# Neighbourhood attention on one Trainium2 core: P is turned and scaled by a product with a diagonal matrix

## The reference

```
q = (gn(x) @ Wq + bq).reshape(B, nh, H, W, lr) * scale      # nh = 8 heads, lr = 4
k = (gn(x) @ Wk + bk).reshape(B, nh, H, W, lr)
v = (gn(x) @ Wv + bv).reshape(B, nh, H, W, hd)              # hd = 32
...
attn = jnp.einsum('bhijc,bhikjlc->bhijkl', q, k_win)        # 7 x 7 keys of each query
attn = attn + bias
attn = jax.nn.softmax(attn.reshape(B, nh, H, W, K * K), axis=-1)
out = jnp.einsum('bhijkl,bhikjld->bhijd', attn, v_win)
x = x + out @ Wp + bp
```

## Time and profile before

| | us |
|---|---|
| median of 3 runs | 10392.46 |
| lowest and highest | 10381.14, 10393.34 |
| span of the profiled execution | 10375.5 |
| `layer0_attend`, clearing of `qn` to last transposes, in it | 374.5 to 2483 |
| PE busy over the span | 8825.9 (85%) |
| DVE, ACT, POOL busy | 5783.3, 4145.5, 3261.0 |
| TensorE clock granted, mean over the span | 0.809 of 2.4 GHz |

### The profile page before, as it was taken

The page is one execution under the profiler, slowest core; times in us unless marked ns, Lnnn a source line. Parts: engine busy times, 40 slices in busy tenths (PEclk is TensorE's granted clock), DMA queues, the critical chain, the costliest instruction groups (busy, mean ns, idle before and its releaser), DMA issues. The chain is left out here.

```text
span 10375.5 us, 158377 instructions
## 1 busy us (share of the span) xinstructions
PE 8825.9 (85%) x47072; PEld 4663.3 (45%) x47072; DVE 5783.3 (56%) x13683; ACT 4145.5 (40%) x9073; POOL 3261.0 (31%) x1854
## 2 busy tenths in 40 slices
PE   4499989997667999998999989999999885448888
PEld 3355545554444444444444444444444334325555
DVE  4355555555557976675766757766676004324444
ACT  1255555553000055555555555555555660001111
POOL 2000000000000055555555555555555670142211
PEclk8655555555876599999999999999999996569999
DMA  4511121101533001202112021111211004211110
GB/s 137 88 20 20 20 35 20 20 8 49 178 123 103 10 20 28 56 21 56 27 24 56 19 56 30 31 45 30 47 28 41 14 5 127 78 40 42 44 34 21
DMA packets 368839, 480.22 MB, mean 46 GB/s; under 512 B 154040, under 2 KB 322362, under 8 KB 354855
## 3 DMA queue, kind: packets, MB, share of 16 engines
q1 hardware_dynamic: 344551, 426.24, 17.0%
q0 software_dynamic: 23424, 43.45, 1.6%
HBM read 298.80 MB, written 180.34 MB: 46 GB/s over the span
## 5 line engine op out<-in xcount | busy, mean ns | idle before, releaser
L1057 POOL TENSOR_TENSOR a_added<-a_P 128x896 f32<-128x896 f32 x1344 | 2805.3, 2107 | 3517.1 <-ACT a_P L1029 3516.8
L935 DVE TENSOR_REDUCE a_tops<-a_ps 128x1 f32<-128x448 f32 x5600 | 3166.2, 632 | 1322.8 <-PE a_ps L843 1319.5
L1029 ACT ACTIVATE a_P<-a_ps 128x448 f32<-128x448 f32 (+1 forms) x5600 | 2610.3, 548 | 2600.3 <-PE a_ps L901 2599.3
L901 PE MATMUL a_ps<-a_qp,a_kp 98*128 98x448 f32 (+1 forms) x5600 | 1946.8, 399 | 171.4 <-DMA a_qp<-scratch_neg 97.9
L843 PE MATMUL a_ps<-a_hk,a_hq 96*128 96x448 f32 (+1 forms) x4900 | 1922.6, 406 | 118.9 <-DMA a_hk<-scratch_k 96.8
L843 PEld LDWEIGHTS a_ps<-a_hk,a_hq 96*128 96x128 f32 (+1 forms) x4900 | 917.7, 188 | 1205.3 <-DVE a_tops L935 1047.2
L901 PEld LDWEIGHTS a_ps<-a_qp,a_kp 98*128 98x128 f32 (+1 forms) x5600 | 1008.0, 189 | 951.7 <-ACT a_P L1029 637.8
L860 PE MATMUL a_ps<-a_P,a_vt 128*32 128x448 f32 (+1 forms) x11200 | 1362.2, 558 | 0.0
L459 DVE CUSTOM_DVE_ANT_0 n_sm<-n_ps,n_bias 112x448 f32<-112x448 f32 x928 | 578.1, 624 | 850.8 <-PE n_ps L390 850.8
L485 ACT ACTIVATE n_P<-n_sm,n_mx 112x448 f32<-112x448 f32 x928 | 620.2, 668 | 845.4 <-DVE n_mx L459 845.4
L400 PE MATMUL n_ps<-n_idn,n_P 112*112 112x112 f32 x3712 | 923.5, 404 | 21.5 <-DVE n_P L466 21.5
(11 more groups left out here) (174 smaller groups left out, 6476.7 us busy)
## 6 DMA issues: line engine op xcount, KB each, us to landing
a_qp<-scratch_q SPq DMA_DIRECT2D x168, 224.0 KB, 3.8
a_hq<-scratch_q SPq DMA_DIRECT2D x84, 392.0 KB, 7.3
a_hk<-scratch_k SPq DMA_DIRECT2D x84, 392.0 KB, 8.6
a_kp<-scratch_k SPq DMA_DIRECT2D x96, 320.0 KB, 4.9
scratch_t<-o_ts SPq DMA_DIRECT2D x8, 3136.0 KB, 13.2
e_w<-in_w SPq DMA_DIRECT2D x16, 1024.0 KB
p_xs<-in_x SPq DMA_DIRECT2D x4, 3136.0 KB, 15.3
scratch_v<-p_vs SPq DMA_DIRECT2D x4, 3136.0 KB, 12.5
```

The costliest lines, as they stand in the source:

```text
L901: pe.matmul(PS[0:rows_of(t), i_s % 3, 0:GW], kp[0:98, hh, 128 * t:128 * t + rows_of(t)], qp[0:98, hh, GW * j:GW * j + GW], start=True, sto ...
L935: dve.tensor_reduce(tops[0:rows_of(t), KT * hh + t, k:k + 1], PS[0:rows_of(t), MAX + i % MAXES, 0:GW], AX_X, ALU.max).then_inc(topped, 1)
L1029: act.activation(P[0:rows_of(t), (2 * n + pair) % (2 * RING), hh % 2, :], PS[0:rows_of(t), (4 * n + hh) % 3, 0:GW], ACT.Exp).then_inc(expe ...
L1057: pool.tensor_tensor(added2[:, a % 6, :, :], P[:, (2 * n + pair) % (2 * RING), :, :], P[:, (2 * n + 2 + pair) % (2 * RING), :, :], ALU.add ...
```

## The change

`idn` is no longer the operand against which `P` is turned. DVE makes, for each unit, a diagonal matrix of the 112 reciprocal row sums: `diag` = `idn` times `rc` per row, 112 x 112, in a ring of `ND` = 4. PE multiplies each 112 x 112 block of the unnormalised `P` with it. The result is the block turned and scaled at once. `P` itself is not scaled any more.

```
-        NSM, NP, NPT = 4, 6, 12
+        NSM, NP, NPT, ND = 4, 6, 12, 4
...
+        diag = sb("diag", [TT, ND, TT])
...
             sp.sem_inc(stored, 16)
+            sp.dma_start(idn[:, :], A["eye"][0:TT, 0:TT]).then_inc(consts, 16)
             sp.wait_ge(zeroed, 2)
             load(0, 0, None)
-            sp.dma_start(idn[:, :], A["eye"][0:TT, 0:TT]).then_inc(consts, 16)
...
                         for c in range(4):
-                            last = pe.transpose(PS[0:TT, BT + m % 3, TT * c:TT * c + TT],
-                                                P[:, m % NP, TT * c:TT * c + TT], idn[:, :])
+                            last = pe.matmul(PS[0:TT, BT + m % 3, TT * c:TT * c + TT],
+                                             P[:, m % NP, TT * c:TT * c + TT], diag[:, m % ND, :],
+                                             start=True, stop=True)
...
+            dve.wait_ge(consts, 16)
             dve.memset(qn[:, :, :], 0.0).then_inc(zeroed, 1)
...
                             dve.wait_ge(inverted, it * U + m + 1)
-                            dve.tensor_scalar(P[:, m % NP, :], P[:, m % NP, :], rc[:, m % 8:m % 8 + 1], None,
+                            if m >= ND:
+                                dve.wait_ge(turned, it * U + m - ND + 1)
+                            dve.tensor_scalar(diag[:, m % ND, :], idn[:, :], rc[:, m % 8:m % 8 + 1], None,
                                               ALU.mult).then_inc(normed, 1)
```

## The result

| | us | ratio to the kernel before |
|---|---|---|
| before, median of 3 runs | 10392.46 | |
| after, median of 3 runs (11170.97 to 11187.22) | 11179.25 | 1.0764 (1.0745 to 1.0784) |

The change makes the kernel slower by 787 us. The forecast was 11080 us, within a range of 10450 to 11200. Direction and mechanism were right; the size was 99 us too small.

The account below looks back on a forecast made before the run. PE was taken as the bound, at 1.2 GHz. 10375.5 + 693 (second instructions) + 1 (head) - 8 (tail) = 11061.5 us, plus 17 from span to median, gave 11080 us; range 10450 to 11200.

Parts of the forecast that it names:

- PE bounds the stage, at 1.2 GHz, and stays there: In the changed stage PE is the bound, DVE and ACT follow it, and the clock stays at 0.50.
- DVE's scaling, and its new wait, cost and save nothing: DVE's shorter instruction lies under PE, and building diag waits on products with three units of slack: both cost nothing.
- quarter to a half of 0.45: Sign in the profile after: DVE's build of diag takes a quarter to a half of 0.45 us.
- Two instructions for one, 0.187 us each, 0.75 us a unit: On PE four transposes become eight instructions; four more at 0.187 us add 0.75 us a unit, 693 us for the stage.
- Head: +1 us, at most +5: At the kernel's start, loading idn first delays DVE's memsets by 0 to 5 us, once; taken as +1.
- Tail: 8 us less: At each iteration's end the clock rises sooner, saving 1 us in each of 8 iterations, bounds 0 to 3.
- The 17 us between span and median: The median of the runs lies 17 us above the profiled span, so 11061.5 us becomes 11078.
- The rival of the high clock, 0.17: In the stage PE's clock rises and stays up, a unit takes 1.5 us, the kernel about 9830 us; chance 0.17.
- The other rivals: On PE, loads stop hiding, about 12470 us, chance 0.03; or each product is one instruction, 10392 us, chance 0.02.
- The estimate of 2080 us: Added stage time on PE if, as a skill page says, transposes are four times faster than products for fp32.
- the 0.13 for some fast iterations: The stage's clock rises in some iterations only, 157 us less for each; chance 0.13, two thirds with at most four.
- the 0.19 for faster: Chance that the whole kernel gets faster by more than 0.2%, summed as 0.17 + 0.02.

Follow-up runs that it names:

- e1: The changed kernel with its four products with diag put back to transposes against idn, output left undivided by the row sums: 10387 us, ratio 1.0003.
- e5: The changed kernel with P and diag in fp32r instead of fp32, one instruction per product: 10333 us, ratio 0.9990.
- e9: The changed kernel with its score product over 32 partitions instead of 16, the others zero: 11126 us, ratio 1.0757.
- e10: The changed kernel with its score product over 64 partitions instead of 16, adding the scores of two head rows: 11125 us, ratio 1.0756.
- e2: The changed kernel with filler products of idn with itself at each iteration's start and behind its first four score products: 10371 us, ratio 0.9988.
- e6: The kernel before with its score product over 128 partitions instead of 16, adding the scores of four head rows: 9724 us, ratio 0.9404.
- e7: The kernel before with its score product over 128 partitions and queries zero-padded by GpSimd, so the result is kept: 9699 us, ratio 0.9381.
- e3: The kernel before with filler products of idn with itself at each iteration's start and behind its first four score products: 10440 us, ratio 1.0056.

## Why the prediction was right, and where it was short

*PE bounds the stage, at 1.2 GHz, and stays there.* Right: 0.50 in the middle of all eight iterations.

*DVE's scaling, and its new wait, cost and save nothing.* Right: e1 measured 1.0003. The build of `diag` takes 0.27 us against the "quarter to a half of 0.45"; it is a little above that.

*Two instructions for one, 0.187 us each, 0.75 us a unit.* Right in count and pace. It was short by the first step of a group: 0.33 us where a transpose had 0.24. The group grew by 1.76 - 0.92 = 0.84 us instead of 0.75, which is 0.09 x 928 = 84 us of the 99 that were missing. The forecast took the pace inside a group for every step and read no row for the first one, although gave it: 0.24 against 0.187 for transposes. The excess belongs to a start whose load is exposed: at 2.4 GHz the first step was 0.19 us behind a 16-row score and 0.10 behind a tall one, where the load began early. But the length of the load does not explain it. The loads of this kernel,

```profile
L401 PEld LDWEIGHTS n_ps<-n_diag,n_P x7424: 258/307/312, 459.9 to 3257.6; 112*112 112x112 f32 x196
```

are as long as those of e5, 307 ns in median, and e5's first step was 0.24 us, that of the transposes, whose loads took 213. So the 0.09 us came with the second instruction; why is not shown. One row was misread on the way: 394 ns is the mean of the value products in the earlier trace rows, that of the transposes is 404, which changes nothing in the sum.

*Head: +1 us, at most +5.* The first score product came at 456.5 in place of 451.1, 5.4 us later, just past the bound. `idn` landed in 1.8 us and the memsets began 2.2 us later; the other 3.2 us came with the bias tables, for which DVE waited 55.7 us at most in place of 52.7.

*Tail: 8 us less.* Not seen. The clock rose only when an iteration's products were over or all but over, as before.

*The 17 us between span and median.* It was 2 us this time. In the stage itself the last value product moved from 2485.0 to 3259.8, 774.8 us. The forecast had 686 for it; by the working above, 84 of the 89 us between go back to the first step. The other 27 us of the span's 801.9 lie in stages that were not touched, 23.5 of them in layer 1's attention. e9 and e10, with the same unit of 2.94 us on another chip, took 11125 us. I take this part as the spread from run to run and chip to chip; nothing here shows a cause.

*The rival of the high clock, 0.17.* Not what happened, but a real state of this kernel: e2 reached it in six iterations of eight. Its unit would have been 1.71 us, not 1.5, for the load behind a 16-row product is exposed there too, and its time 10392 - 928 x 0.39, about 10030 us, an estimate, instead of 9830. That the kernel would not get there by itself was a choice between two values and not worked out, so that it came out is in part luck. Whether transposes count less for the clock is not settled: alone they raised it, in e6 and e7 it rose and stayed with them in the loop, and in e3 it fell back with them where e2 held it with products.

*The other rivals.* Loads hid, but for the first one. Plain products were two instructions. The estimate of 2080 us, from a factor of four, did not come: the same four blocks took 1.76 us as products and 0.92 as transposes, a factor of 1.9. In the chances, a third of the 0.13 for some fast iterations, 0.04, is a kernel faster than before, and the 0.19 for faster counts only 0.02 of it.

## What to carry to other kernels

Before a transpose is folded into a product, count its instructions in the trace: a plain fp32 product is two where a transpose is one, and on an engine that is the bound the second costs its full time, whatever another engine saves. Then read the granted clock of the stage. In the changed kernel a unit took 2.94 us at one level and 1.71 at the other, some 1140 us over 928 units, an estimate, which is more than the change itself cost. The clock changed with other instructions in the loop, so an edit that adds work can pay (the tall score on padded queries, 10342 to 9699 us, together with the load that starts early), and one that takes work away can lose (fp32r on the padded changed kernel, 9859 to 10093 us). And cost the first instruction of a group by its own row, not by the pace inside the group.

## What was not expected of the hardware

- The weight load behind a score product of 16 or 64 rows started when that product was done (0.41 us after its start at 2.4 GHz with 16 rows, 0.64 at 1.2 GHz with 16 and 64). Behind one of 128 rows it started 0.09 to 0.14 us after it.
- One kernel held either clock through 116 units of the same instructions, 2.94 us or 1.71 us each (e2). The iterations differed in what had come before the units.
- An fp32r product of 112 columns took its turn every 0.187 us at 1.2 GHz, as slow as a half of a plain fp32 product or a transpose.
